# Reciprocals of the softmax sums spread over a tile by two transposes a step instead of four float32 products

## What is computed

```python
x = _layernorm(x + _L0_attn_ref(x, ...))   # 16 heads of 64, queries and keys over the 256 tokens of a row
x = _layernorm(x + _L0_ffn_ref(x, ...))    # shared expert + top 2 of 8 experts
x = _layernorm(x + _L1_attn_ref(x, ...))   # "attention" among the 16 heads of one token, 8 wide
x = _layernorm(x + _L1_ffn_ref(x, ...))    # top 2 of 8 experts
```

```python
weights = jnp.einsum('bqhd,bkhd->bhqk', q, kf)
weights = jax.nn.softmax(weights, axis=-1).astype(dtype)
new_vals = jnp.einsum('bhqk,bkhd->bqhd', weights, v).astype(dtype)
```

## Time and profile before

| What | us |
|---|---|
| median of 3 runs | 1473.27 (1472.85 to 1474.88) |
| the profiled execution, its own time | 1472.66 |
| its span, first to last instruction | 1470.9 |
| TensorE busy | 1395.0 (95%) |
| VectorE busy | 942.5 (64%) |
| ScalarE busy | 865.2 (59%) |
| GpSimd busy | 515.5 (35%) |
| L1032, the four products a step, busy | 84.5 (1024 records) |
| L659, the reciprocals, busy | 21.5 (128) |

### The profile page before, as it was taken

How to read it: one execution, slowest core, us unless ns; L and a number is a source line. 1 busy time by engine, 2 the same in 40 slices (tenths; PEclk the granted TensorE clock), 3 DMA queues, 4 the chain that set the end, 5 groups by cost and what they waited for, 6 DMA issues and landing times.

```text
span 1470.9 us, 34497 instructions
## 1 busy us (share of the span) xinstructions
PE 1395.0 (95%) x12096; PEld 1237.2 (84%) x12096; DVE 942.5 (64%) x2534; ACT 865.2 (59%) x2361; POOL 515.5 (35%) x415
## 2 busy tenths in 40 slices
PE   5897999999999999999999999999999999999837
PEld 4685989898898989989898898989889898988737
DVE  4456575775766667576666757677575667757482
ACT  4565756656575565657656565765757566574303
POOL 2307052350705325070532607043260704416140
PEclk9899999999999999999999999999999999999978
DMA  7000000000000000000000000000000000000000
GB/s 255 5 2 5 1 2 8 0 7 0 0 7 0 7 0 7 0 0 7 0 7 0 7 1 0 7 0 7 0 1 6 0 7 0 4 2 1 5 4 4
DMA packets 14089, 13.78 MB, mean 9 GB/s; under 512 B 1626, under 2 KB 12771, under 8 KB 13795
## 3 DMA queue, kind: packets, MB, share of 16 engines
q1 hardware_dynamic: 14050, 13.27, 2.8%
HBM read 11.17 MB, written 2.10 MB: 9 GB/s over the span
## 4 chain that ended last, share of the span: by engine, by line
PE 68%; issue 12%; DVE 10%; POOL 4%; ACT 3%; POOLq 2%; DVEq 1%; DMA 0%; SPq 0%; ACTq 0%
PE bank_F L1100 16%; PE bank_S L982 5%; PE bank_T L1011 4%; PE bank_A L1039 4%; PE bank_A L1024 3%; PE bank_T L968 3%; DVE hid L742 3%; PE bank_T L969 3%; PE bank_T L970 3%; PE bank_A L1032 3%; PE bank_A L969 3%; PE bank_A L968 3%; PE bank_A L970 3%; PE bank_F L968 2%; DVE neg_max L651 2%
## 5 line engine op out<-in xcount | busy, mean ns | idle before, releaser
L1100 PE MATMUL bank_F<-down,hid 128*128 128x128 f32 x3072 | 373.5, 277 | 16.3 <-DVE x L730 15.6
L1100 PEld LDWEIGHTS bank_F<-down,hid 128*128 128x128 f32 x3072 | 357.9, 192 | 25.5 <-DVE x L730 16.6
L543 ACT ACTIVATE probs<-bank_S,neg_max 128x256 f32<-128x256 f32 x512 | 236.0, 475 | 168.1 <-DVE neg_max L651 168.1
L651 DVE TENSOR_REDUCE neg_max<-bank_S 128x2 f32<-128x512 f32 x256 | 164.6, 684 | 72.8 <-PE bank_S L982 69.8
L471 POOL TENSOR_TENSOR hid<-hid,qkv 128x1024 f32<-128x1024 f32 x62 | 177.0, 2867 | 39.8 <-ACT hid L559 39.8
L730 DVE SCALAR_TENSOR_TENSOR x<-bank_F,gates,x 128x128 f32<-128x128 f32 x512 | 154.9, 344 | 47.8 <-PE bank_F L1100 37.6
L522 ACT ACTIVATE probsT<-bank_T 128x512 f32<-128x512 f32 x256 | 139.6, 605 | 47.0 <-PE bank_T L1011 46.9
L441 POOL TENSOR_TENSOR mean_sq<-sum_sq,one_over_d 128x2 f32<-128x2 f32 x16 | 3.2, 197 | 448.6 <-ACT h_row L517 448.6
L1011 PE MATMUL bank_T<-ident,probs 128*128 128x128 f32 x1024 | 138.2, 278 | 0.2 <-ACT probs L543 0.2
L459 POOL TENSOR_TENSOR hid<-qkv 128x1024 f32<-128x1024 f32 x47 | 112.2, 2388 | 66.7 <-ACT qkv L522 66.7
L1011 PEld LDWEIGHTS bank_T<-ident,probs 128*128 128x128 f32 x1024 | 112.2, 141 | 25.5 <-issue 21.3
(11 more groups left out here) (167 smaller groups left out, 3194.7 us busy)
## 6 DMA issues: line engine op xcount, KB each, us to landing
x_row<-in_x SPq DMA_DIRECT2D x16, 128.0 KB, 2.1
down<-in_w SPq DMA_DIRECT2D x1, 2048.0 KB, 15.2
out<-x SPq DMA_DIRECT2D x16, 128.0 KB, 1.8
hid<-in_w SPq DMA_DIRECT2D x1, 1536.0 KB, 7.8
hid<-in_rw SPq DMA_DIRECT2D x1, 1024.0 KB, 7.4
hid<-in_wv SPq DMA_DIRECT2D x1, 512.0 KB, 3.8
hid<-in_wq SPq DMA_DIRECT2D x1, 512.0 KB, 4.7
hid<-in_wk SPq DMA_DIRECT2D x1, 512.0 KB, 5.5
```

The lines of the kernel that those rows point to most:

```text
L543: ins = sc.activation(probs[:, h // 2 % 2, h % 2, t, :], unit.bank(f"S{h}")[:, t * S:(t + 1) * S], ACT.Exp, bias=neg_max[:, h, t:t + 1], a ...
L651: ve.tensor_reduce(neg_max[:, h, :], v.bank(f"S{h}")[:, :].rearrange("p (t k) -> p t k", t=NT), AX.X, ALU.max, negate=True).then_inc(max_r ...
L1100: ins = te.matmul(bank[:, (j * NT + t) * P:(j * NT + t + 1) * P], hid[:, e, k, tokens(t)], down[:, e, k, :], start=k == 0, stop=k == m - 1)
```

## The change

The reciprocals go to `sum_inv`; a copy on VectorE repeats each of them 64 times along the row into `row_inv` (128 partitions, 2 halves of the tokens, 2 heads, 64), and only then `inverse_ready` is raised. On TensorE, `spread` transposes each half of `row_inv`, 128 by 128, into the bank's columns 256 to 511: two transposes in place of four products. `spread(v, s)` waits for the bank's last tenant and for `inverse_ready`. For steps 0 to 5 it is issued in front of the score pair S(2s+4), S(2s+5), thus one score pair earlier than the products were; for O6 and O7 it stays in front of the unit's own products. `x2` becomes another name of `x1` and `ao` one of `h_row`; VectorE now waits for `x2plus_ready` before it writes the next row's residual.

```diff
--- before.py
+++ after.py
@@ -230,13 +230,14 @@
         probs = sb("probs", P, 2, 2, NT, S)
         probsT = sb("probsT", P, 2, NT, S)
         row_sum = sb("row_sum", P, 2, 2 * NT)
-        row_inv = sb("row_inv", P, 2, 2 * NT)
+        sum_inv = sb("sum_inv", P, 2, 2 * NT)
+        row_inv = sb("row_inv", P, 2, NT, 2, DH)
         oT = sb("oT", P, HP, S)
         x1 = sb("x1", P, NT, D)
         x1T = split("x1T_hi", P, S), split("x1T_lo", P, S)
         hid0 = sb("hid0", P, E + 1, M0, S)
 
-        x2 = sb("x2", P, NT, D)
+        x2 = x1
         x2T = sb("x2T", P, S)
         gates0T = x2T[0:E + 1, :]
         aoT = x3T = x2T
@@ -251,7 +252,7 @@
         pv1 = prod.rearrange("p t h (d x) c -> p t h d (x c)", d=DH1)
         sum1 = sb("sum1", P, NT, NH1)
         inv1 = sb("inv1", P, NT, NH1)
-        ao = sb("ao", P, NT, NH1, DH1)
+        ao = h_row[:].rearrange("p t (h d) -> p t h d", h=NH1)
         x3 = sb("x3", P, NT, D)
         x3T_parts = x1T
         hid1 = sb("hid1", P, E, M1, S)
@@ -656,7 +657,9 @@
                 unit = v.previous() if s == 0 else v
                 for j in range(2):
                     dve.wait_ge(*unit.drain(f"S{2 * s + j}"))
-                settled(dve, ve.reciprocal(row_inv[:, s % 2, :], row_sum[:, s % 2, :]).then_inc(inverse_ready, 1))
+                settled(dve, ve.reciprocal(sum_inv[:, s % 2, :], row_sum[:, s % 2, :]))
+                source = sum_inv[:, s % 2].rearrange("p (j t a) -> p t j a", j=2, a=1)
+                settled(dve, ve.tensor_copy(row_inv[:, s % 2], source.broadcast_to([P, NT, 2, DH])).then_inc(inverse_ready, 1))
 
             def o_scale(v, s):
 
@@ -873,6 +876,8 @@
                 if v.a:
                     o_scale(v, HP - 1)
                     dve.wait_ge(xplus_ready, v.at(0, 1, 1))
+                    if v.b:
+                        dve.wait_ge(x2plus_ready, v.at(1, 1, 1))
                     residual(v, "OUT", x1, x_plus)
                     ln_stats(v, 0, x1)
                 if v.b:
@@ -983,6 +988,14 @@
                                             start=n == 0, stop=n == 2)
                             if (t, n) == (NT - 1, 2):
                                 ins.then_inc(v.fill(f"S{2 * s + j}")[0], 1)
+
+            def spread(v, s):
+
+                bank = v.bank(f"O{s}")
+                pe.wait_ge(*v.drain(f"O{s}", before=1))
+                pe.wait_ge(inverse_ready, v.at(0, HP, s + 1))
+                for t in range(NT):
+                    te.transpose(bank[:, S + t * P:S + (t + 1) * P], row_inv[:, s % 2, t].rearrange("p j e -> p (j e)"), ident[:])
 
             def unit(v, name):
                 bank = v.bank(name)
@@ -1025,12 +1038,8 @@
                     return ins
                 if name[0] == "O":
                     s = int(name[1:])
-                    pe.wait_ge(inverse_ready, v.at(0, HP, s + 1))
-                    for t in range(NT):
-                        for j in range(2):
-                            n = j * NT + t
-                            te.matmul(bank[j * DH:j * DH + DH, S + t * P:S + (t + 1) * P],
-                                      row_inv[:, s % 2, n:n + 1].broadcast_to([P, DH]), ident[:], start=True, stop=True)
+                    if s >= HP - 2:
+                        spread(v, s)
                     for j in range(2):
                         pe.wait_ge(*v.drain(f"T{2 * s + j}"))
                     for k in range(NT):
@@ -1106,7 +1115,7 @@
                     return te.matmul(bank[:, 0:3 * D], x2T[:, tokens(t)], wqkv1[:], start=True, stop=True)
                 if name == "AOT":
                     pe.wait_ge(ao_ready, v.at(1, NT, NT))
-                    return transpose_row(bank, ao[:].rearrange("p t h d -> p t (h d)"))
+                    return transpose_row(bank, h_row)
                 assert name == "PROJ"
                 wait_drained(v, name, "AOT")
                 for t in range(NT):
@@ -1115,6 +1124,8 @@
 
             def body(v):
                 for name, bank in (pe_units(v.it) if v.it >= 0 else PRE):
+                    if name[0] == "S" and bank == "S0" and v.nth.get(f"O{int(name[1:]) // 2 - 2}"):
+                        spread(v, int(name[1:]) // 2 - 2)
                     free, count = v.drain(name, before=1)
                     if v.it > 0 or count:
                         pe.wait_ge(free, count)
```

## The result

| | us |
|---|---|
| after, median of 4 runs | 1510.79 (1509.67 to 1512.34) |
| before, median of 4 runs beside them | 1474.08 (1472.85 to 1477.24) |
| ratio | 1.0246 (95% interval 1.0227 to 1.0266) |
| the profiled execution of after, its own time and span | 1512.34, 1510.5 |

The kernel is 2.5% slower. The forecast had the sign and most of the mechanism, but 1489 us, and the range ended at 1500: the measured time lies outside it. Between the two profiled executions there are 39.7 us (1512.34 less 1472.66), of which the forecast explains 16.

A forecast was written before the change was run, and what follows sets the result against it. VectorE's and ScalarE's chain was taken to bound some 16 us of each 86.30 us pass, TensorE 70; 1.5 + 0.3 - 0.8 = +1.0 a pass over 15 rows, plus 1 for the first, gave 1489 us, range 1464 to 1500.

The forecast's parts named there:

- Part 3's step on copy 5: Behind step 5's reciprocal: the copy waits 2.4 us for GpSimd, which then goes first; VectorE's second-attention product ends 1.4 later.
- The stand at S14: At the score pair of S14: TensorE stands 1.3 us, because the exponentials that free its banks come later.
- The hold of copy 7: Behind O6, after the last reciprocal: GpSimd's L466 makes the copy hold VectorE for 1.1 us.
- The copy's own duration: Each step's 128x256 float32 copy on VectorE: 0.29 us, plus a gap of 0.10; free in steps 0 to 4.
- The shared buffers and the x2plus wait: Sharing h_row and waiting for x2plus before the residual: cost nothing.
- O0, O1 and O2 give 3 x -0.27 = -0.8 us: From OUT to the next S10: TensorE sets the pace, so transposes for products save 0.27 us at each of three steps.
- O6 starts 1.5 us later.: VectorE's chain in front of O6: held copies start L760 1.7 us later, less 0.17 already waited there today.
- The walk to the sums: From step 5's reciprocal to VectorE's sums of L760: held copies start them 1.7 us later, 642.45 instead of 640.72.
- OUT and its last eighth come +0.3 us late, net.: Behind O6: TensorE gains about 0.4 us, VectorE loses 1.1 to 1.4 against 1.24 of cover; net +0.3 us.
- The first row and pass 1: First row +1 us, between -2 and +3; pass 1 counted among the 15 rows at +1.0 us each.
- it is worse: Rival, 12%: VectorE's loss behind O6 is handed on, or the clock falls in stands; up to 1 us more a pass, 1504 us.
- The copy never stands: Rival, 13%: the copy never waits for GpSimd, taking 0.42 + 0.10 us; -0.3 us a pass, 1468 us.

The follow-up runs named there:

- never-held form: The whole change with the copy written as a reduction over one element, against the changed kernel: 1490.53 us, ratio 1.0123 to the kernel before.
- the kernel with half the sum: The changed kernel without copies, reciprocals replaced by a constant, and VectorE's sum of D0p2 leaving out one of two experts: 1465.07 us, ratio 0.9948.

## Why the prediction was wrong

**What held.** Part 3's step on copy 5: held to the end of L460 (forecast 2.4 us, measured 2.44), L467 then ahead of the product, its end 1.4 later. The stand at S14 (forecast 1.3; 0.76 + 0.38 in the time line). The hold of copy 7 (1.1; 1.02). The copy's own duration (0.29; 0.294) and its being free in steps 0 to 4. The shared buffers and the x2plus wait cost nothing: the kernel with only the copy has them, and its S2 to S12 is before's. The kernel with the never-held form confirms the mechanism by taking it away.

**The step that failed first: "O0, O1 and O2 give 3 x -0.27 = -0.8 us".** Measured +0.04. Three errors. A step saves 0.21 on the array and not 0.27 (S6-S8, S8-S10). The account from OUT to S10 forgot that the fourth pair of transposes, O3's, had moved into this stretch with its 0.22, so the array's own balance was about -0.4 (-0.46 in the kernel with half the sum). And the 0.5 that the products of O0 take in step 1 was not TensorE's to save: S4-S6 is set by VectorE's sum of D0p2, without any slack. I had read "TensorE idles 0.29 us" as "TensorE sets the pace everywhere else". The kernel with half that sum shows the 0.5. This one term is 0.8 us a pass, 12 us.

**"O6 starts 1.5 us later."** From S12 to O6's own first record it is 10.92 us before (634.96 to 645.88) and 12.76 after (655.00 to 667.76): +1.84. The walk to the sums held: 7.33 us behind the reciprocal of step 5 before (633.39 to 640.72), 9.10 after (653.45 to 662.55), +1.77 where I had 1.7, although copy 6 was free (L460, 3.32 us long beside the product's tail, moved L467 to the end just in front of it). But the 0.17 in front of the second sum, which I took off because L466 would be done, stayed as an issue gap, and some 0.1 came with it. Term mis-sized by 0.3.

**"OUT and its last eighth come +0.3 us late, net."** Nearly right, at another place: the shorter O6 and O7 give 0.35 and OUT's start loses 0.35, so the head of OUT comes out even. The last eighth waits a second time, for the scaling of O7, as the chain of waits and the time line of VectorE after show:

```profile
675.28 3.39 PE bank_A L1037 x28
678.68 0.71 PE bank_A L1037 x4
```

```profile
677.44 0.69 DVE L780 TENSOR_REDUCE h_row<-hid 128x64 f32<-128x512 f32 x1 [0.17 <-issue]
678.20 0.42 DVE L667 TENSOR_TENSOR oT<-oT,bank_A 128x256 f32<-128x256 f32 x1
```

VectorE, late by copy 7, has a part of the second attention in front of that scaling. OUT-S2 is +0.42: 0.1 more than the term.

Together: forecast +1.0 a pass; the three steps add 0.84, 0.3 and 0.1, which makes 2.2, and the measured sum is 2.24.

**The first row and pass 1.** I took +1 and the steady +1.0; measured +2.9 and +6.1. In pass 1 the same two copies are held as in a steady pass, 5 and 7. But in the kernel before VectorE's product had been the first there, 0.15 us ahead of GpSimd, and had cost 1.27 us instead of 3.26; with the copy in front it lost that place:

```profile
116.56 1.27 DVE L742 TENSOR_TENSOR hid<-qkv 128x1024 f32<-128x1024 f32 x1
116.71 3.33 POOL L459 TENSOR_TENSOR hid<-qkv 128x1024 f32<-128x1024 f32 x1
```

```profile
120.28 2.37 POOL L460 TENSOR_TENSOR hid<-qkv 128x1024 f32<-128x1024 f32 x1
120.33 2.47 DVE L662 COPY row_inv<-sum_inv 128x256 f32<-128x256 f32 x1
122.89 2.25 DVE L745 TENSOR_TENSOR hid<-qkv 128x1024 f32<-128x1024 f32 x1
```

S12-S14 is 2.8 us longer there (4.59 to 7.38), not 1.2. The prediction walked one steady pass and took it for all 15. Besides, the granted clock falls in TensorE's stands, which the prediction had named under "it is worse". The stretch view of pass 1, before and after:

```profile
127.00:138.00 11.00, 8.58 (x75) 6.74 (x75) 6.19 (x13) 5.56 (x16) 10.72 (x6) 1.00 0.01 1
138.00:173.60 35.60, 32.03 (x238) 29.94 (x239) 18.33 (x62) 22.52 (x49) 4.46 (x6) 0.95 0.02 5
```

```profile
134.00:147.00 13.00, 10.04 (x60) 7.54 (x59) 7.16 (x13) 5.19 (x15) 11.91 (x6) 0.74 0.00 0
147.00:182.80 35.80, 32.95 (x248) 30.58 (x247) 18.78 (x63) 22.75 (x49) 2.99 (x6) 0.95 0.02 5
```

With the copy alone pass 1 is 87.83 and with the transposes behind the pair 87.94, so some 4 of the 6.1 us are the copies', and the fall of the clock is among them: with the copy alone OUT takes 5.47 us at a granted clock of 0.69, in after 5.52 at 0.68, before 3.84 at 1.00. The last 2 us come with the transposes in front of the pair. One stand of 0.53 there (120.22, for the bank's last scaling) is the wait that the prediction had said ends in time; the others are not taken apart. The first row's 2.9 stays open: three copies are held in it (3.69, 1.60 and 3.24 us), but the kernel with the copy alone does that row in 68.77, less than before.

**The rivals.** "The copy never stands" fell with the rows of copies 5 and 7. Its price was wrong too: I gave 1468 for a copy of 0.42, the kernel that has one took 1490.53. Of the 1.2 us a pass between the two, 0.8 are the same term from S2 to S10; behind O6, where I had booked -0.4, it has +0.5. "It is worse", 1504, named as its cause VectorE's loss behind O6 handed on, and the clock: both were there, the clock in the first row and pass 1 only, and it deserved more than 12%.

## What to carry to other kernels

An engine at 95% with 0.3 us of idle time in a pass can still be tied to others at several places: before booking a saving, look at each bank it comes to in that stretch and by how much the tenant before was drained ahead of it. A walk through one steady pass does not price the passes written out ahead of the loop. A float32 copy within SBUF on VectorE beside GpSimd's elementwise work is priced by when it starts, not by its size; a reduction over one element did the same work in 0.42 us and was never held, and moving a product of two SBUF inputs out of GpSimd's way was worth more than the edit under study. When an edit moves the time by tens of us and the profile says "issue", look at the packets of the instruction queue before believing any story of the edit itself.

## What the runs showed of the hardware that I had not expected

- Where a loop body lies in TensorE's instruction stream can cost 1.4 to 6.6 us a turn (passes 2 to 13 of three kernels, each against the last turn of the same kernel): 127 idle instructions ahead of the loop made 1473 us into 1496, 63 of them turned 1513 into 1461, and the instruction queue's packets (24 or 132) tell which case it is. Only turns that another follows pay.
- Whichever of VectorE and GpSimd starts first has priority, down to 0.07 us either way: GpSimd first at 653.62 against 653.69, the copy takes 2.44; GpSimd first at 633.55 against 633.73, the product takes 3.26; VectorE first at 627.64 against 627.71, it takes 1.23 and GpSimd's operation 3.37 instead of 2.36.
- A repeated source (one element read 64 times) does not take a copy out of its fast form: 256 elements a partition took 0.293 us where a reduction over one element took 0.420. The Trainium skill (VectorE: DVE Perf Modes, perf-mode tier table) gives float32 copies within SBUF the double rate; the rows agree. The Trainium skill (SBUF — State Buffer, "Who interferes with whom") also says that a `tensor_reduce` never contends with GpSimd on this chip: 128 of 128 within 2 ns agree with it.
- A change of array shape on TensorE is not free: the same two transposes save 0.21 us on four products in front of the score pair and 0.07 behind it.
